# A second buffer for the small softmax weights, and ScalarE's exponentials ahead of its copies within each place

## The chip, the core and the metric

The kernel runs on one core of one Trainium2 chip. The metric is device time in microseconds (us), the median of several runs. Engines go by the profile's names: PE is TensorE (PEld its weight loads), ACT is ScalarE, DVE is VectorE, POOL is GpSimd, SP is the queue that issues the DMAs. "SPq", "ACTq" are the sequencers of those engines.

## The reference

A layer norm feeds two branches that are added to the input: latent attention and an int8 quantised feed-forward layer. What matters here is the attention:

```python
kv_c = x @ W_kv_down;  q_c = x @ W_q_down          # latents, rank 64 and 192
q = concat(q_c @ W_q_nope, rope(q_c @ W_q_rope))   # 16 heads
k = concat(kv_c @ W_k_nope, rope(kv_c @ W_k_rope)) # 4 key heads, each for 4 query heads
attn = softmax(where(causal, -inf, q @ k.T * scale))
out = (attn @ v) @ W_o                             # 2 sequences of 1024 tokens
```

## The kernel before

Each engine has its own program, written out by hand; the engines meet only at semaphores, and each works strictly through its list. After about 90 us of preparation comes the attention loop of 32 **steps** (n = 0 to 31), each one query head over one sequence of 1024 tokens, and then the feed-forward layer from about 760 us. The work of a step is cut into 7 **places** (j = 0 to 6).

The 1024 queries of a step are 8 tiles of 128 rows. Tile i sees (i + 1) * 128 keys. `UNITS` gives the tiles that a place handles: 7, 3, 6, 2, 5, then 1 and 0 together, then 4. Tiles 7, 6, 5, 4 are **big**: their scores alternate between two pairs of PSUM banks. Tiles 3, 2, 1, 0 are **small**: they all share one PSUM bank, so each small place can only be scored when DVE has finished with the one before it.

For one tile: PE forms the scores (`scores`, L1214); DVE takes the row maximum (`maxima`, L864); ACT exponentiates twice, once to an f16 high part in SBUF (L679 big, L684 small) and once in place in PSUM (L680, L685); DVE subtracts to get the f16 low part (`big_low` L872, `small_low` L879). Then SP turns the weights with DMA transposes (`turn_big` L358, `turn_small` L367) and PE multiplies them with the values one step later (tiles 6, 5, 4 and the small ones) or at place 6 of the same step (tile 7).

The high and low parts of all four small tiles of a step lie in one buffer, `p_small`, and go through one DMA transpose into `pt_small`. So the first small exponential of step n (tile 3, place 1) waits until the transpose of step n - 1 has landed (`small_in`, L683). That transpose is issued after the last `small_low` of step n - 1, which DVE does at the end of place 6.

Beside this, PE fills a bank `misc` with side work whose results another engine copies out; each new entry of `misc` waits for the copy of the last (`misc_used`). `misc_of(n)` lists it. With r = n % 4:

- every step (up to n = 29): two halves of a query for step n + 2, places 3 and 5, copied out by ACT (`query`, L608). POOL then rotates them.
- r = 0 or 2 (n from 2; 15 steps, below called **turn steps**): two transposes of normalised heads, `turn` 1 at place 5 and `turn` 0 at place 6. ACT copies each out (`turn_high`, L665) and DVE then makes the low part (`turn_low`, L898).
- r = 1 and r = 2 (n over 4): output products, two in each such step, added up by DVE (`add_out`); ACT has no part in them.
- in steps 0, 1, 3, 4, 7, 8, 11, 12 some extra entries (`EXTRA`): integer weights and activations that ACT copies out, and keys.

In the text, step 16 is the one whose first exponential starts at 432.54 us; it has r = 0. Step 17 starts at 454.39 and step 18 (r = 2) at 474.74.

Within place j, the lists read so. PE: scores of the place, products with values, then the `misc` entries. DVE at place 5: maxima of tiles 1 and 0, normalisation, low part of tile 5, `turn_low` 1. DVE at place 6: maximum of tile 4, `turn_low` 0, then `small_low` of tiles 1 and 0. At places 0 to 2 of the next step: maximum of 7, low part of 4, maximum of 3, maximum of 6, low part of 7, `small_low` of 3. ACT (L687 to L707): first the copies out of `misc` of the place, then its exponentials. PE's scores of tile 3 wait for `small_low` of tile 0, those of tile 6 for the low part of tile 4 of the step before, those of tile 2 (place 3) for `small_low` of tile 3.

Of the kernel before, what the change touches and what calls it, by code (L numbers as in the profile page):

```python
# [20 lines left out]
P = 128  # L21
# [26 lines left out]
F32, F32R, F16, BF16, U32 = (mybir.dt.float32, mybir.dt.float32r, mybir.dt.float16, mybir.dt.bfloat16,  # L48
                             mybir.dt.uint32)
ALU, ACT, AX = mybir.AluOpType, mybir.ActivationFunctionType, mybir.AxisListType  # L50
# [14 lines left out]
COLS = {7: 0, 5: 0, 6: 2 * CH, 4: 2 * CH + P, 3: 4 * CH, 2: 4 * CH, 1: 4 * CH, 0: 4 * CH + 2 * P}  # L65
KEYS = {7: (CH, CH), 6: (CH, CH - P), 5: (CH, 2 * P), 4: (CH - P, 2 * P), 3: (CH,), 2: (CH - P,), 1: (2 * P,), 0: (2 * P,)}

OFF = {3: 0, 2: 4 * P, 1: 7 * P, 0: 9 * P}
WB = 10 * P
# [5 lines left out]
QHI_SLOT = 4  # L75
# [11 lines left out]
LAST = HKV * STEPS  # L87


def misc_of(n):  # L90

    r, usual = n % REP, []
    if n + 2 < LAST:
        usual += [(3, "query", 0), (5, "query", 1)]
    if n < LAST:
        if r in (0, 2) and n >= 2:
            usual += [(5, "turn", 1), (6, "turn", 0)]
        if r == 1 and n > REP:
            usual += [(4, "out", 0), (6, "out", 1)]
        if r == 2 and n > REP:  # L100
            usual += [(2, "out", 2), (4, "out", 3)]
    return sorted(usual + EXTRA.get(n, []), key=lambda x: x[0])
# [8 lines left out]
def misc_index(n, kind, k):  # L111

    return MISC_BASE + MISC_AT[n, kind, k]


def build(nc, x, w_kv_down, w_k_nope, w_k_rope, w_v, w_q_down, w_q_nope, w_q_rope, w_o, w1, b1, w2, b2,
          cos_rows, sin_rows, out):
    with ExitStack() as ctx:
        def sb(name, shape, dt, where=ctx):
            return where.enter_context(nc.sbuf_tensor(name, shape, dt))  # L120

        def sem(name):
            return ctx.enter_context(nc.semaphore(name))
# [40 lines left out]
        psum = ctx.enter_context(nc.psum_tensor("psum", [P, 8 * CH], F32))  # L164
# [45 lines left out]
        att = ExitStack()  # L210
# [2 lines left out]
        q_raw = [sb(f"q_raw{i}", [P, T], F32, att) for i in range(2)]  # L213
        q_lo = [sb(f"q_lo{i}", [P, T], F32R, att) for i in range(2)]
        q_hi = [sb(f"q_hi{i}", [P, T], F32R, att) for i in range(2)]
        p_small = sb("p_small", [P, 2 * WB], F16, att)
        pt_small = sb("pt_small", [P, len(BLOCKS), P], F16, att)
        p_src = [sb(f"p_src{i}", [P, 2, T], F16, att) for i in range(PSRC)]
        pt_big = {i: sb(f"pt_big{i}", [P, 2 * (i + 1), P], F16, att) for i in BIG}
# [31 lines left out]
        S = {n: sem(n) for n in names}  # L251
# [27 lines left out]
        def _(sp):  # L279
# [87 lines left out]
            def turn_small(n):  # L367

                if n:
                    sp.wait_ge(S["pv_done"], PV_STEP * n)  # L370
                sp.wait_ge(S["small_lo"], len(SMALL) * (n + 1))
                sp.dma_start(pt_small[:, :, :], p_small[:, :], transpose=True).then_inc(S["small_in"], 16)

            for g in range(HKV):
                for s in range(STEPS):
                    n = STEPS * g + s
# [146 lines left out]
        def _(act):  # L523
# [84 lines left out]
            def query(n, s, idx, k):  # L608
                act.wait_ge(S["misc_full"], idx + 1)
                if k == 0 and n is not None:  # L610
                    act.wait_ge(S["qlo_done"], n - 1)
                act.activation(q_raw[s % 2][:, k * CH:(k + 1) * CH], misc[:, :], ACT.Copy, scale=SCALE)\  # L612
                   .then_inc(S["misc_used"], 1)

            def query_high(n, s):
                act.wait_ge(S["rotated"], n + 1)
                act.activation(q_hi[n % 2][:, :], q_raw[s % 2][:, :], ACT.Copy).then_inc(S["qhi_done"], 1)  # L617
# [6 lines left out]
            def turned_integers(kind, k, idx):  # L624
                act.wait_ge(S["misc_full"], idx + 1)
                if kind == "x":
                    ins = act.activation(qx_t[:, k % 2, k // 2 * CH:(k // 2 + 1) * CH], misc[:, :], ACT.Copy, bias=-MAGIC)
                elif k < 2:
                    ins = act.activation(w1_t[:, k, :], misc.bitcast(BF16), ACT.Copy)
                else:  # L630
                    ins = act.activation(w2_t[:, 4 * (k - 2):4 * (k - 1), :],
                                         misc.bitcast(BF16).rearrange("p (t n) -> p t n", n=D), ACT.Copy)
                ins.then_inc(S["misc_used"], 1)
# [35 lines left out]
            def exponentials(n, u):  # L669

                for i in UNITS[u]:
                    w, nb = (i + 1) * P, sm["mcol"][:, NT * (n % 2) + i:NT * (n % 2) + i + 1]
                    src = psum[:, COLS[i]:COLS[i] + w]
                    act.wait_ge(S["max_done"], NT * n + MAX_AT[UNITS[u][-1]] + 1)
                    if i in BIG:
                        q = NB * n + BIG[i]
                        if q >= PSRC:
                            act.wait_ge(p_in[q % PSRC], 32 * (q // PSRC))
                        act.activation(p_src[q % PSRC][:, 0, 0:w], src, ACT.Exp, bias=nb).then_inc(S["hi_done"], 1)  # L679
                        act.activation(src, src, ACT.Exp, bias=nb).then_inc(S["exp_done"], 1)  # L680
                    else:
                        if n:
                            act.wait_ge(S["small_in"], 16 * n)  # L683
                        act.activation(p_small[:, OFF[i]:OFF[i] + w], src, ACT.Exp, bias=nb)  # L684
                        act.activation(src, src, ACT.Exp, bias=nb).then_inc(S["small_exp"], 1)  # L685

            for n in range(LAST + 1):  # L687
                s = n % STEPS
                for j in range(NS):
                    for slot, kind, k in misc_of(n):  # L690
                        if slot != j:
                            continue
                        idx = misc_index(n, kind, k)
                        if kind == "query":
                            query(n + 2, s + 2, idx, k)
                        elif kind in ("w", "x"):
                            turned_integers(kind, k, idx)
                        elif kind == "turn":
                            turn_high(1 if s % REP == 0 else 0, k, idx)
                    if n == LAST:  # L700
                        continue
                    if j == QHI_SLOT and n + 1 < LAST:
                        query_high(n + 1, s + 1)
                    exponentials(n, j)
                    for slot, kind, k in misc_of(n):
                        if slot == j and kind == "kb":
                            keys_high(k)  # L707
            act.activation(sm["gelu"], sm["half"][:, 0:1], ACT.Gelu)

# [27 lines left out]
        def _(dve):  # L737
# [141 lines left out]
            def small_low(n, i):  # L879

                o, w = OFF[i], (i + 1) * P
                dve.wait_ge(S["small_exp"], len(SMALL) * n + SMALL[0 if i == 1 else i] + 1)
                dve.tensor_tensor(p_small[:, WB + o:WB + o + w], psum[:, COLS[i]:COLS[i] + w], p_small[:, o:o + w],  # L883
                                  ALU.subtract).then_inc(S["small_lo"], 1)

            def normalise(m, half):
# [89 lines left out]
            for n in range(LAST + 1):  # L976
                s, r = n % STEPS, n % REP
                for j in range(NS):
# [36 lines left out]
                    if n < LAST and j == 6:  # L1015
                        small_low(n, 1)
                        small_low(n, 0)
# [6 lines left out]
            for i in range(16):  # L1024
# [5 lines left out]
                if i in OUT_AT:  # L1030
                    k = OUT_AT[i]
# [424 lines left out]
```

## Time and profile before

| | |
|---|---|
| three runs | 828.88, 833.61, 837.66 us; median 833.61 |
| the profiled execution | 825.37 us, of which its span 823.6 us |
| mean granted TensorE clock | 0.915 |
| PE busy | 653.2 us (79%) |
| DVE busy | 551.5 us (67%) |
| ACT busy | 503.1 us (61%) |
| POOL busy | 417.7 us (51%) |

The span runs from the first to the last instruction of the profiled execution; the rest of its time lies around it. Busy shares are means over preparation, the attention loop and the feed-forward layer. In the loop no engine is busy throughout, so the waits between them decide.

### The profile page before, as it was taken

How to read it: one execution, taken by the hardware profiler on the slowest of the kernel's cores; microseconds unless marked ns; L12 is line 12 of the kernel's file. 1: busy time of each engine (PE TensorE's matmuls, PEld its weight loads, DVE VectorE, ACT ScalarE, POOL GpSimd, SP SyncE). 2: the span in 40 equal slices, each digit the busy share in tenths (PEclk: the TensorE clock that was granted, in tenths of full speed). 3: DMA queues.
4: the chain of work that ended last, by engine and by line, in shares of the span. 5: the costliest groups of instructions: out<-in, count | busy, mean ns of one | idle time of the engine just before them, and what ended most of it. 6: DMA issues, size and time to landing. Idle time of an engine off the chain costs nothing.

```text
span 823.6 us, 15788 instructions
## 1 busy us (share of the span) xinstructions
PE 653.2 (79%) x6282; PEld 509.1 (62%) x6282; DVE 551.5 (67%) x890; ACT 503.1 (61%) x759; POOL 417.7 (51%) x208
## 2 busy tenths in 40 slices
PE   8885778887888798878887887788877877886766
PEld 6663556665666576656765675566666755674535
DVE  6746687766677667765765677566665756676696
ACT  4556765676566656665666666566665657665553
POOL 2411656565566555564656565555564646540225
PEclk9776897999999999998989999999999999998879
DMA  9762468777958756785767758777676757668102
GB/s 274 239 215 119 84 131 143 128 145 174 179 97 150 146 113 110 155 148 120 129 116 141 117 116 149 134 129 129 123 133 112 120 97 133 118 117 147 30 1 103
DMA packets 323609, 108.34 MB, mean 132 GB/s; under 512 B 305808, under 2 KB 314576, under 8 KB 323408
## 3 DMA queue, kind: packets, MB, share of 16 engines
q1 hardware_dynamic: 322752, 106.74, 66.0%
q8 instruction: 50, 0.82, 0.4%
q10 hardware_dynamic: 784, 0.59, 0.3%
q14 instruction: 23, 0.19, 0.1%
HBM read 21.30 MB, written 10.49 MB: 39 GB/s over the span
## 4 chain that ended last, share of the span: by engine, by line
PE 49%; DVE 21%; DMA 14%; ACT 10%; issue 5%; POOL 0%; SPq 0%; POOLq 0%; ACTq 0%; DVEq 0%
PE psum L1077 45%; DMA pt_small<-p_small 11%; DVE small L868 5%; DVE p_small L883 3%; DVE p_src L876 3%; ACT psum L685 2%; DMA pt_big<-p_src 2%; PE psum L1275 2%; ACT p_src L679 2%; ACT psum L680 1%; DVE hid L1057 1%; ACT q_raw L612 1%; ACT p_small L684 1%; DVE kt_a L963 1%; DVE small L1026 1%
## 5 line engine op out<-in xcount | busy, mean ns | idle before, releaser
L868 DVE TENSOR_REDUCE small<-psum 128x1 f32<-128x1024 f32 (+7 forms) x256 | 188.9, 752 | 84.9 <-PE psum L1077 84.8
L486 POOL TENSOR_TENSOR q_lo<-q_raw,q_hi 128x1024 fp32r<-128x1024 f32 x32 | 76.5, 2390 | 242.0 <-ACT q_hi L617 242.0
L1077 PE MATMUL psum<-k_hi,q_hi 128*128 128x512 f32 (+2 forms) x384 | 165.4, 431 | 26.0 <-DVE p_src L876 18.0
L679 ACT ACTIVATE p_src<-psum,small 128x1024 f16<-128x1024 f32 (+3 forms) x128 | 122.1, 954 | 80.3 <-DVE small L868 79.8
L876 DVE TENSOR_TENSOR p_src<-psum,p_src 128x1024 f16<-128x1024 f32 (+3 forms) x128 | 130.0, 1016 | 12.5 <-ACT psum L680 12.4
L1077 PE MATMUL psum<-k_lo,q_hi 128*128 128x512 f32 (+2 forms) x384 | 135.7, 353 | 0.0
L1077 PE MATMUL psum<-k_hi,q_lo 128*128 128x512 f32 (+2 forms) x384 | 135.7, 353 | 0.0
L1077 PE MATMUL psum<-cmask,ident 128*128 128x128 bf16 x256 | 59.4, 232 | 87.9 <-DVE p_small L883 87.0
L680 ACT ACTIVATE psum<-psum,small 128x1024 f32<-128x1024 f32 (+3 forms) x128 | 118.5, 926 | 0.0
L883 DVE TENSOR_TENSOR p_small<-psum,p_small 128x512 f16<-128x512 f32 (+3 forms) x128 | 59.5, 486 | 86.0 <-ACT psum L685 85.1
L1077 PE MATMUL psum<-kv_tok,pt_big 128*128 128x65 f16 (+1 forms) x2496 | 106.8, 200 | 8.5 <-DMA pt_big<-p_src 8.4
L1077 PEld LDWEIGHTS psum<-kv_tok,pt_big 128*128 128x128 f16 x2496 | 90.7, 102 | 31.3 <-issue 20.9
L1077 PEld LDWEIGHTS psum<-cmask,ident 128*128 128x128 bf16 x256 | 24.7, 97 | 130.5 <-DVE p_small L883 93.9
L684 ACT ACTIVATE p_small<-psum,small 128x512 f16<-128x512 f32 (+3 forms) x128 | 67.8, 530 | 60.2 <-DMA pt_small<-p_small 50.6
L1077 PEld LDWEIGHTS psum<-k_hi,q_hi 128*128 128x128 f32 x384 | 78.1, 203 | 42.3 <-DVE p_src L876 27.5
L471 POOL TENSOR_TENSOR q_swap<-q_raw,sin_sb 32x1024 f32<-32x1024 f32 x31 | 73.4, 2368 | 48.3 <-ACT q_raw L612 33.8
L612 ACT ACTIVATE q_raw<-psum 128x512 f32<-128x512 f32 x64 | 38.3, 599 | 91.7 <-PE psum L1077 91.7
L1077 PEld LDWEIGHTS psum<-k_hi,q_lo 128*128 128x128 f32 x384 | 75.6, 197 | 7.5
L1077 PEld LDWEIGHTS psum<-k_lo,q_hi 128*128 128x128 f32 x384 | 76.7, 200 | 2.3
L480 POOL TENSOR_TENSOR q_raw<-q_raw,q_swap 64x1024 f32<-64x1024 f32 x31 | 74.7, 2410 | 2.4
L474 POOL TENSOR_TENSOR q_swap<-q_raw,sin_sb 32x1024 f32<-32x1024 f32 x31 | 73.9, 2384 | 2.4
L477 POOL TENSOR_TENSOR q_raw<-q_raw,cos_sb 64x1024 f32<-64x1024 f32 x31 | 73.3, 2363 | 2.4
(164 smaller groups left out, 1154.9 us busy)
## 6 DMA issues: line engine op xcount, KB each, us to landing
wq_split<-w_split SPq DMA_DIRECT2D x4, 1024.0 KB, 5.4
k_rotated<-k_split SPq DMA_DIRECT2D x8, 512.0 KB, 3.4
wq<-wq_split SPq DMA_DIRECT2D x16, 256.0 KB, 3.1
pt_big<-p_src SPq DMA_TRANSPOSE x256, 3.1
acc<-in_L_attn_x SPq DMA_DIRECT2D x4, 512.0 KB, 7.5
ffn_t<-in_L_attn_W_o SPq DMA_DIRECT2D x1, 2048.0 KB, 20.0
k_hi<-k_rotated SPq DMA_DIRECT2D x8, 256.0 KB, 4.0
k_lo<-k_rotated SPq DMA_DIRECT2D x8, 256.0 KB, 4.5
```

What stands on the lines that cost most here:

```text
L471: pool.tensor_tensor(q_swap[0:HR, :], raw[HR:ROPE, :], sin_sb[HR:ROPE, :], ALU.mult)\
L474: pool.tensor_tensor(q_swap[HR:ROPE, :], raw[0:HR, :], sin_sb[0:HR, :], ALU.mult)\
L477: pool.tensor_tensor(raw[0:ROPE, :], raw[0:ROPE, :], cos_sb[0:ROPE, :], ALU.mult)\
L480: pool.tensor_tensor(raw[0:ROPE, :], raw[0:ROPE, :], q_swap[:, :], ALU.add).then_inc(S["pool_step"], 1)
L486: pool.tensor_tensor(q_lo[s % 2][:, :], q_raw[s % 2][:, :], q_hi[n % 2][:, :], ALU.subtract)\
L679: act.activation(p_src[q % PSRC][:, 0, 0:w], src, ACT.Exp, bias=nb).then_inc(S["hi_done"], 1)
L680: act.activation(src, src, ACT.Exp, bias=nb).then_inc(S["exp_done"], 1)
L684: act.activation(p_small[:, OFF[i]:OFF[i] + w], src, ACT.Exp, bias=nb)
L868: dve.tensor_reduce(sm["mcol"][:, NT * (n % 2) + i:NT * (n % 2) + i + 1], psum[:, COLS[i]:COLS[i] + (i + 1) * P], AX.X, ALU.max, negate=True)\
L876: dve.tensor_tensor(p_src[q % PSRC][:, 1, 0:w], psum[:, COLS[i]:COLS[i] + w], p_src[q % PSRC][:, 0, 0:w], ALU.subtract).then_inc(S["lo_don ...
L883: dve.tensor_tensor(p_small[:, WB + o:WB + o + w], psum[:, COLS[i]:COLS[i] + w], p_small[:, o:o + w], ALU.subtract).then_inc(S["small_lo"], 1)
L1077: ins = pe.matmul(dst, lhs, rhs, start=start, stop=stop, skip_group_check=True)
```

## The change

Two edits. First, `p_small` becomes two buffers, used in turn by the parity of the step; the first small exponential of step n now waits for the transpose of step n - 2. `pt_small`, the transpose itself and its place in SP's list stay as they are. Second, ACT does the exponentials of a place first (preceded at place 4 by `query_high`, as before) and then the copies out of `misc`; the keys' high part stays behind the exponentials.

```diff
-        p_small = sb("p_small", [P, 2 * WB], F16, att)
+        p_small = [sb(f"p_small{k}", [P, 2 * WB], F16, att) for k in range(2)]
...
-                sp.dma_start(pt_small[:, :, :], p_small[:, :], transpose=True).then_inc(S["small_in"], 16)
+                sp.dma_start(pt_small[:, :, :], p_small[n % 2][:, :], transpose=True).then_inc(S["small_in"], 16)
...
-                        if n:
-                            act.wait_ge(S["small_in"], 16 * n)
-                        act.activation(p_small[:, OFF[i]:OFF[i] + w], src, ACT.Exp, bias=nb)
+                        if n >= 2:
+                            act.wait_ge(S["small_in"], 16 * (n - 1))
+                        act.activation(p_small[n % 2][:, OFF[i]:OFF[i] + w], src, ACT.Exp, bias=nb)
...
             for n in range(LAST + 1):
                 s = n % STEPS
                 for j in range(NS):
+                    if n < LAST:
+                        if j == QHI_SLOT and n + 1 < LAST:
+                            query_high(n + 1, s + 1)
+                        exponentials(n, j)
                     for slot, kind, k in misc_of(n):
                         if slot != j:
                             continue
...
                             turn_high(1 if s % REP == 0 else 0, k, idx)
-                    if n == LAST:
-                        continue
-                    if j == QHI_SLOT and n + 1 < LAST:
-                        query_high(n + 1, s + 1)
-                    exponentials(n, j)
-                    for slot, kind, k in misc_of(n):
-                        if slot == j and kind == "kb":
+                        elif kind == "kb":
                             keys_high(k)
...
-                dve.tensor_tensor(p_small[:, WB + o:WB + o + w], psum[:, COLS[i]:COLS[i] + w], p_small[:, o:o + w],
+                dve.tensor_tensor(p_small[n % 2][:, WB + o:WB + o + w], psum[:, COLS[i]:COLS[i] + w], p_small[n % 2][:, o:o + w],
```

The lists of PE, DVE, SP and POOL keep their order. ACT's changes. In a turn step, ACT's places 5 and 6 read like this before: the second half of a query is copied (`q_raw`), then `turn` 1 (`o_hi`), then the exponentials of tiles 1 and 0 (`p_small` is a high part in SBUF, `psum` the one in place), then `turn` 0, then tile 4.

```order
L612 ACTIVATE q_raw<-psum 128x512 [waits misc_full]
L667 ACTIVATE o_hi<-psum 128x512 [waits misc_full]
L684 ACTIVATE p_small<-psum,small 128x256 [waits small_in,max_done]
L685 ACTIVATE psum<-psum,small 128x256
L684 ACTIVATE p_small<-psum,small 128x128 [waits small_in,max_done]
L685 ACTIVATE psum<-psum,small 128x128
L667 ACTIVATE o_hi<-psum 128x512 [waits misc_full]
L679 ACTIVATE p_src<-psum,small 128x640 [waits p_in2,max_done]
L680 ACTIVATE psum<-psum,small 128x640
```

The same two places of ACT now:

```order
L684 ACTIVATE p_small<-psum,small 128x256 [waits small_in,max_done]
L685 ACTIVATE psum<-psum,small 128x256
L684 ACTIVATE p_small<-psum,small 128x128 [waits small_in,max_done]
L685 ACTIVATE psum<-psum,small 128x128
L612 ACTIVATE q_raw<-psum 128x512 [waits misc_full]
L667 ACTIVATE o_hi<-psum 128x512 [waits misc_full]
L679 ACTIVATE p_src<-psum,small 128x640 [waits p_in2,max_done]
L680 ACTIVATE psum<-psum,small 128x640
L667 ACTIVATE o_hi<-psum 128x512 [waits misc_full]
```

The exponentials of tiles 1 and 0 moved ahead of two copies, and the copy of `turn` 0 moved behind those of tile 4. DVE's list at the same places, the same before and now, is what takes from these: low part of tile 5, `turn_low` 1 (`o_lo`), maximum of tile 4, `turn_low` 0, `small_low` of tiles 1 and 0, then the maximum of tile 7 of the next step and the low part of tile 4.

```order
L876 TENSOR_TENSOR p_src<-psum,p_src 128x768 [waits exp_done]
L901 TENSOR_TENSOR o_lo<-psum,o_hi 128x512 [waits o_hi_done]
L868 TENSOR_REDUCE small<-psum 128x1 [waits score_done]
L901 TENSOR_TENSOR o_lo<-psum,o_hi 128x512 [waits o_hi_done]
L883 TENSOR_TENSOR p_small<-psum,p_small 128x256 [waits small_exp]
L883 TENSOR_TENSOR p_small<-psum,p_small 128x128 [waits small_exp]
L868 TENSOR_REDUCE small<-psum 128x1 [waits score_done]
L876 TENSOR_TENSOR p_src<-psum,p_src 128x640 [waits exp_done]
```

Nothing moved here. At place 3 of every step with a query, ACT had the copy of its first half ahead of tile 2; this is before:

```order
L612 ACTIVATE q_raw<-psum 128x512 [waits qlo_done,misc_full]
L684 ACTIVATE p_small<-psum,small 128x384 [waits small_in,max_done]
L685 ACTIVATE psum<-psum,small 128x384
L617 ACTIVATE q_hi<-q_raw 128x1024 [waits rotated]
L679 ACTIVATE p_src<-psum,small 128x768 [waits p_in2,max_done]
```

And the same place of ACT now:

```order
L684 ACTIVATE p_small<-psum,small 128x384 [waits small_in,max_done]
L685 ACTIVATE psum<-psum,small 128x384
L612 ACTIVATE q_raw<-psum 128x512 [waits qlo_done,misc_full]
L617 ACTIVATE q_hi<-q_raw 128x1024 [waits rotated]
L679 ACTIVATE p_src<-psum,small 128x768 [waits p_in2,max_done]
```

The two exponentials of tile 2 moved ahead of the copy; `query_high` and tile 5 follow as before.

## Rows read from the trace of the kernel before

**Rows 1.** The page, part 4: the chain that ended last, by line.

```profile
PE psum L1077 45%; DMA pt_small<-p_small 11%; DVE small L868 5%; DVE p_small L883 3%; DVE p_src L876 3%; ACT psum L685 2%; DMA pt_big<-p_src 2%; PE psum L1275 2%; ACT p_src L679 2%; ACT psum L680 1%; DVE hid L1057 1%; ACT q_raw L612 1%; ACT p_small L684 1%; DVE kt_a L963 1%; DVE small L1026 1%
```

**Rows 2.** Waits: who waited for whom, us in total, times, longest.

```profile
POOL q_lo L486 <- ACT q_hi L617: 242.0, 32, 13.9
...
PE psum L1077 <- DVE p_small L883: 87.0, 34, 4.8
...
ACT p_small L684 <- DMA pt_small<-p_small: 50.6, 24, 3.6
```

**Rows 3.** Timeline, step 16, places 0 to 3: start, us, engine, [idle before <-releaser].

```profile
433.55 1.08 ACT L680 ACTIVATE psum<-psum,small 128x1024 f32<-128x1024 f32 x1
...
435.95 1.22 DVE L876 TENSOR_TENSOR p_src<-psum,p_src 128x1024 f16<-128x1024 f32 x1
...
436.70 0.69 ACT L684 ACTIVATE p_small<-psum,small 128x512 f16<-128x512 f32 x1 [2.07 <-DMA pt_small<-p_small]
...
437.97 0.69 DVE L883 TENSOR_TENSOR p_small<-psum,p_small 128x512 f16<-128x512 f32 x1 [0.80 <-ACT psum L685]
...
438.72 0.29 PE L1077 MATMUL psum<-cmask,ident 128*128 128x128 bf16 x1 [3.24 <-DVE p_small L883]
```

**Rows 4.** Groups by line and shape: busy us, mean ns, idle before, releaser.

```profile
L883 DVE TENSOR_TENSOR p_small<-psum,p_small 128x512 f16<-128x512 f32 x32 | 22.0, 688 | 16.7 <-ACT psum L685 16.4
...
L883 DVE TENSOR_TENSOR p_small<-psum,p_small 128x384 f16<-128x384 f32 x32 | 17.9, 558 | 68.9 <-ACT psum L685 68.7
```

**Rows 5.** Timeline, step 16 (r = 0), places 5 and 6, ACT.

```profile
447.74 0.60 ACT L612 ACTIVATE q_raw<-psum 128x512 f32<-128x512 f32 x1
449.14 0.60 ACT L667 ACTIVATE o_hi<-psum 128x512 fp32r<-128x512 f32 x1 [0.81 <-PE psum L1275]
449.64 0.47 ACT L684 ACTIVATE p_small<-psum,small 128x256 f16<-128x256 f32 x1
...
450.60 0.36 ACT L685 ACTIVATE psum<-psum,small 128x128 f32<-128x128 f32 x1
451.37 0.60 ACT L667 ACTIVATE o_hi<-psum 128x512 fp32r<-128x512 f32 x1 [0.41 <-PE psum L1275]
451.87 0.79 ACT L679 ACTIVATE p_src<-psum,small 128x640 f16<-128x640 f32 x1
452.54 0.77 ACT L680 ACTIVATE psum<-psum,small 128x640 f32<-128x640 f32 x1
```

**Rows 6.** Timeline, the same stretch, DVE.

```profile
445.17 1.48 DVE L868 TENSOR_REDUCE small<-psum 128x1 f32<-128x768 f32 x3
...
450.38 0.81 DVE L868 TENSOR_REDUCE small<-psum 128x1 f32<-128x640 f32 x1
452.00 0.69 DVE L901 TENSOR_TENSOR o_lo<-psum,o_hi 128x512 fp32r<-128x512 f32 x1 [0.81 <-ACT o_hi L667]
452.61 0.61 DVE L883 TENSOR_TENSOR p_small<-psum,p_small 128x256 f16<-128x256 f32 x2
453.14 1.22 DVE L868 TENSOR_REDUCE small<-psum 128x1 f32<-128x1024 f32 x1
```

**Rows 7.** Timeline, step 17, PE: the scores of tiles 6 and 2.

```profile
455.14 0.50 PE L1077 MATMUL psum<-k_hi,q_hi 128*128 128x512 f32 x1 [0.82 <-DVE p_src L876]
...
460.35 0.23 PE L1077 MATMUL psum<-cmask,ident 128*128 128x128 bf16 x1 [3.02 <-DVE p_small L883]
```

**Rows 8.** Timeline, step 18 (r = 2), place 5, ACT and DVE.

```profile
487.37 0.62 DVE L868 TENSOR_REDUCE small<-psum 128x1 f32<-128x256 f32 x2 [0.26 <-PE psum L1077]
...
488.63 0.60 ACT L612 ACTIVATE q_raw<-psum 128x512 f32<-128x512 f32 x1 [0.59 <-PE psum L1077]
```

**Rows 9.** Windows: us, busy of each engine, PEclk, DMA share, GB/s.

```profile
412.44:432.54 20.10, 16.44 (x162) 12.98 (x162) 12.42 (x21) 12.47 (x20) 9.89 (x5) 0.83 0.67 119
495.28:513.27 17.99, 13.91 (x162) 10.94 (x162) 12.32 (x21) 12.47 (x20) 9.59 (x5) 1.00 0.87 153
...
99.00:760.00 661.00, 535.08 (x5617) 424.51 (x5615) 444.53 (x713) 416.65 (x641) 366.03 (x156) 0.94 0.72 132
```

## The prediction

> **What bounds the kernel now.** I read the chain that ended last first, for the engine and the stall on it: PE's matmuls (L1077) are 45% of the span and the transpose of the small weights is 11%, by far the largest piece that is not computing [rows 1]. Next the waits, for who is late to whom: ACT idles 50.6 us in 24 places for that transpose, and PE idles 87.0 us in 34 places for `small_low` (L883), mostly before the scores of tile 2 [rows 2]. So the naive reading is that one buffer costs up to 50.6 us. Then I read one such stall in time order, because a wait is worth only what the next engine does with it.
>
> In step 16 ACT is done with tile 7 at 433.55 + 1.08 = 434.63, could start tile 3 then, and starts at 436.70 [rows 3]. But DVE takes tile 3 only after the low part of tile 7, which ends at 435.95 + 1.22 = 437.17. It started `small_low` at 437.97, with 0.80 us of true idle before it, and PE followed at 438.72 after 3.24 us idle [rows 3]. Of ACT's 2.07 us wait, PE can get 0.80 back. The rest is covered by DVE, whose own work since the scores of tile 6 is the true chain to PE.
>
> **The second buffer (term A).** Over the kernel, DVE's idle before `small_low` of tile 3 is 16.7 us, of which ACT is blamed for 16.4 [rows 4]. With two buffers ACT can be ready before DVE in every step: from 434.63, two exponentials up to the 1.27 us that lie between 436.70 and DVE's start at 437.97 end at 435.90, ahead of 437.17 [rows 3]. So A = -16.4 us. Its bounds are 0 (something else late takes its place) and -50.6 us (all of ACT's wait [rows 2]); I take the DVE row, since PE waits for DVE and not for ACT. The transpose still goes out at the same time, so what SP has queued behind it (the two transposes of tile 4, for PE's products right after the scores of tile 2) gets no earlier.
>
> The Trainium skill speaks for the change: the page "Trainium Kernel Development and Optimization", section Best Practices, tells to double-buffer so that DMA overlaps with compute. By it the DMA wait would vanish, 50.6 us; by DVE's idle row it is worth 16.4 us here, since another engine stands between the buffer and PE.
>
> **Exponentials first at place 3.** Today DVE idles 68.7 us before `small_low` of tile 2 [rows 4], about 2.1 us in each of 32 steps, because ACT waits for the query's matmuls and copies before it exponentiates. The new order removes most of that. What is behind it on DVE is the maximum of tile 5, then the maxima of 1 and 0 that wait for PE's next scores; and PE's wait row for L883 counts 34 stalls in 32 steps, about one a step, the one at tile 2 [rows 2, 7]. PE does not wait for tile 2's low part (which gates tiles 1 and 0). I cost it at nothing: PE's own queue of matmuls hides it. The copy comes later by the two exponentials only where PE's matmuls were done before; POOL, which takes queries onward, idles 242.0 us [rows 2], 7.6 us a step, and hides a delay of under 2 us.
>
> **Exponentials first at places 5 and 6 of a turn step (term B).** Here DVE's list alternates with ACT's: `turn_low` 1, maximum of 4, `turn_low` 0, `small_low` 1 and 0, maximum of 7. Step 16 by its rows [rows 5, 6]:
>
> - Maxima of 5, 1, 0 end at 445.17 + 1.48 = 446.65. New: the four exponentials start there. They took 449.64 to 450.60 + 0.36 = 450.96, so 1.32 us; the copy of the query can start about 447.9 against 447.74 now. All that follows up to `turn_low` 1 and the maximum of 4 shifts by 0.1 to 0.2 us.
> - The maximum of 4 ends at 450.38 + 0.81 = 451.19, now near 451.35. New: ACT does tile 4 at once, two activations of 0.67 us start to start (451.87 to 452.54), and only then the copy of `turn` 0: 451.4 + 1.35 = 452.75, where it was 451.37. Shift 1.4 us.
> - DVE waits for that copy to do `turn_low` 0 (452.00) and, behind it, `small_low` 1 and 0 (452.61) and the maximum of 7 (453.14). All shift by 1.4 us. No idle lies before the maximum of 7 in which it could be lost.
> - PE's scores of tile 3 wait for that `small_low`; those of tile 6 wait for the low part of 4, right behind the maximum of 7, and already waited (455.14, 0.82 idle) [rows 7]. Then maximum of 6, low part of 7, `small_low` 3, scores of 2: the stall of 3.02 us at 460.35 [rows 7] stays, 1.4 us later, less the gain of A.
>
> For r = 2 the first point is worse. Maxima of 1 and 0 end at 487.37 + 0.62 = 487.99 and the copy of the query starts at 488.63 [rows 8]; new it starts at 487.99 + about 1.25 = 489.25, 0.6 us later, so `turn_low` 1 is 0.6 us later and the total 0.6 + 1.25 = 1.85 us. There are 7 turn steps with r = 0 and 8 with r = 2: B = 7 x 1.4 + 8 x 1.85 = 24.6 us. Bounds: 15 x 0.8 = 12 us, if the 0.8 us idle ahead of tile 6 swallows part, and 15 x 2.1 = 32 us, if both copies are delayed by both pairs.
>
> **Smaller terms.** C: a few transposes land late (longest ACT wait 3.6 us against 2.07 in step 16 [rows 2, 3]). Where this falls on the step after a turn, tile 4's transposes, queued on SP behind an even later small one, keep PE from its products, so about 1.5 us of A is lost twice: 3 us, between 0 and 5. D: twelve copies of integer activations and weights in steps 0 to 4 fall behind exponentials. Where two `misc` entries follow each other PE waits for the copy; a pair of 0.67 us activations is 1.3 us. I take three such delays, 4 us, between 0 and 12 x 1.3 = 16 us. The feed-forward part is not touched.
>
> **Sum.** -16.4 + 24.6 + 3 + 4 = +15.2 us. Against the profiled execution: 825.4 + 15.2 = 840.6 us, 1.8% more. The median of the three runs is 833.6, 1.0% over that execution, so I forecast 833.6 + 15.2 = 849 us.
>
> **TensorE's clock.** The granted clock was 0.94 over the loop [rows 9], a mix of the two levels 1.2 and 2.4 GHz: (1 - 0.94) / 0.5 x 661 = 79 us at the lower. Two steps with the same work show its price: 20.10 us at 0.83 and 17.99 us at 1.00, so 6.8 us at 1.2 GHz cost 2.1 us [rows 9]; by that rate the loop pays 79 x 0.31 = 24 us. The idle before tile 2 shrinks (3.24 to about 2.4 us) while new idle before tile 3 comes up in turn steps. I take no change, and half of the 24 us either way as the bound. The Trainium skill, page "TensorE: Matmul & The Clock Gate", section "Why this matters for your kernels", says that idle gaps between bursts of matmuls bring the lower clock. The stall of 3.24 us fits it, with a slower mask (0.29 us) behind it [rows 3]; the one of 3.02 us, with 0.23 us behind it [rows 7], does not.
>
> **The rivals.**
>
> 1. The buffer decides (faster). If the copy of `turn` 0 slips without delaying DVE, only A is left: 833.6 - 16.4 = 817 us, and it would be lower still by the double-buffering rule. For it: 11% of the chain is this transpose [rows 1]. Against it: DVE stands idle for exactly that copy (0.81 us at 452.00 [rows 6]). It decides from the point where the shift of a turn step is under (16.4 - 7) / 15 = 0.6 us. Chance 0.12.
> 2. The clock gives back (no change). Shorter stalls keep 2.4 GHz longer and save 12 us: 833.6 + 3 = 837 us. For it: the longest stalls are the ones that shrink. Against it: a turn step has more idle in all. Chance 0.16.
> 3. The clock takes more. Each turn step has a stall at tile 3, at tile 6 and at tile 2 within a few us, and the lower clock is granted 12 us' worth more: 861 us. Chance 0.15.
> 4. Half and half: turn steps lose only 0.8 us each and A is whole, D small: -16.4 + 12 + 4 = 0, so 834 us. Chance 0.07.
>
> **Numbers.** The forecast (841 to 858 us) has 0.50. Time over 1% either way (under 825.3 or over 841.9) is about what a measurement of this kernel can tell from no change. Faster is rival 1 and a sliver of rival 2: 0.13. Same is the rest of rival 2 and rival 4: 0.22. Slower is the forecast and rival 3: 0.65. The range leaves out rival 1 and the far end of rival 3: 829 to 863 us. The forecast's own range is 841 to 858.
>
> **What the changed profile would show.** A right: no ACT wait for `pt_small` left, and DVE's idle before `small_low` 128x512 near 0; PE's stall before tile 2 near 2.4 us. B right: in turn steps `o_hi` of `turn` 0 starts 1.3 us or more behind the maximum of 4, behind both activations of 128x640; DVE's waits for `o_hi` grow from 0.8 us to over 2 us in each; PE shows a new stall before the scores of tile 3. Place 3 right: the 68.7 us of DVE idle before 128x384 shrink by more than half, and the time shows nothing of it. The forecast is wrong if DVE turns out to have slack behind `turn_low` 0, if tile 2's earliness shortens the way to place 5 by more than the copies lose, or if the granted clock over the loop moves away from 0.94.

## The result

The changed kernel takes 858.76 us (median of 4 runs, 854.11 to 860.86) against 832.59 us before: the ratio is 1.030, 95% interval 1.023 to 1.0375. It is slower by 26 us; the forecast was 849 us, slower by 15. The profiled execution took 857.32 us, its span is 855.5 us, its mean granted clock 0.892 where it was 0.915. In the experiments below, times are medians, and executions that ran slow at a lower granted clock are left out of them.

The page of the changed kernel, part 4 (the chain that ended last, by line). From L706 of the kernel before on, the line numbers are lower by 2: L881 is `small_low`, L874 `big_low`, L866 the maxima, L899 `turn_low`, L1075 the matmuls, L1273 the `turn` transposes.

```profile
PE psum L1075 47%; DVE small L866 11%; DVE p_src L874 6%; DVE p_small L881 3%; ACT psum L680 2%; DVE o_lo L899 2%; DMA pt_big<-p_src 2%; ACT o_hi L667 2%; DVE hid L1055 1%; PE psum L1273 1%; ACT psum L685 1%; ACT q_raw L612 1%; ACT p_small L684 1%; DVE small L1024 1%; DVE kt_a L961 1%
```

The transpose of the small weights, 11% in [rows 1], has left the chain. DVE's maxima and low parts stand in its place. The waits of the changed kernel (us in total, times, longest):

```profile
PE psum L1075 <- DVE p_small L881: 79.1, 44, 4.7
DVE o_lo L899 <- ACT o_hi L667: 58.2, 31, 2.0
...
PE psum L1273 <- ACT q_raw L612: 21.8, 14, 2.4
...
PE psum L1324 <- ACT ffn_t L627: 6.5, 3, 2.8
```

PE's wait for `small_low` fell only from 87.0 us to 79.1, and it now comes 44 times instead of 34 [rows 2]: twelve of them are stalls of about 1 us before the scores of tile 3, by the timeline. `turn_low` now waits 58.2 us for ACT's copies; in the kernel before, this wait and the one of `turn`'s transposes for the copy of the query were:

```profile
DVE o_lo L901 <- ACT o_hi L667: 25.8, 28, 1.3
...
PE psum L1275 <- ACT q_raw L612: 16.0, 14, 1.4
```

Two groups of the changed kernel by line and shape, the ones that answer to [rows 4] (busy, mean ns, idle before):

```profile
L881 DVE TENSOR_TENSOR p_small<-psum,p_small 128x512 f16<-128x512 f32 x32 | 21.7, 679 | 0.0
...
L881 DVE TENSOR_TENSOR p_small<-psum,p_small 128x384 f16<-128x384 f32 x32 | 17.8, 557 | 2.7
```

Both idle times, 16.7 and 68.9 us before, are gone, as the two edits mean them to be. The kernel is slower all the same.

### The profile page after: what moved, and what is told of

It reads as the page before. It is cut to its first block, busy times and chain, and to the rows that moved or that the text cites. A ratio compares the mean times of both kernels' runs of the same rounds, so it can differ in the third digit from the quotient of the medians.

```text
span 855.5 us, 15781 instructions
## 1 busy us (share of the span) xinstructions
PE 673.9 (79%) x6279; PEld 521.8 (61%) x6282; DVE 552.1 (65%) x890; ACT 507.5 (59%) x759; POOL 416.5 (49%) x208
## 4 chain that ended last, share of the span: by engine, by line
PE 50%; DVE 30%; ACT 11%; issue 5%; DMA 3%; SPq 0%; POOL 0%; POOLq 0%; DVEq 0%; ACTq 0%
PE psum L1075 47%; DVE small L866 11%; DVE p_src L874 6%; DVE p_small L881 3%; ACT psum L680 2%; DVE o_lo L899 2%; DMA pt_big<-p_src 2%; ACT o_hi L667 2%; DVE hid L1055 1%; PE psum L1273 1%; ACT psum L685 1%; ACT q_raw L612 1%; ACT p_small L684 1%; DVE small L1024 1%; DVE kt_a L961 1%
## 5 line engine op out<-in xcount | busy, mean ns | idle before, releaser
L866 DVE TENSOR_REDUCE small<-psum 128x1 f32<-128x1024 f32 (+7 forms) x256 | 190.2, 753 | 156.5 <-PE psum L1075 154.9
L1075 PE MATMUL psum<-k_hi,q_hi 128*128 128x512 f32 (+2 forms) x384 | 170.1, 443 | 25.8 <-DVE p_src L874 17.8
L1075 PE MATMUL psum<-k_lo,q_hi 128*128 128x512 f32 (+2 forms) x384 | 139.4, 363 | 0.0
L1075 PE MATMUL psum<-k_hi,q_lo 128*128 128x512 f32 (+2 forms) x384 | 139.4, 363 | 0.0
L874 DVE TENSOR_TENSOR p_src<-psum,p_src 128x1024 f16<-128x1024 f32 (+3 forms) x128 | 129.7, 1013 | 1.4 <-ACT psum L680 1.4
L1075 PE MATMUL psum<-cmask,ident 128*128 128x128 bf16 x256 | 60.5, 236 | 79.1 <-DVE p_small L881 79.1
L1075 PE MATMUL psum<-kv_tok,pt_big 128*128 128x65 f16 (+1 forms) x2496 | 107.2, 200 | 9.4 <-DMA pt_big<-p_src 9.3
L1075 PEld LDWEIGHTS psum<-kv_tok,pt_big 128*128 128x128 f16 x2496 | 91.1, 102 | 33.4 <-issue 18.6
L1075 PEld LDWEIGHTS psum<-k_hi,q_hi 128*128 128x128 f32 x384 | 81.4, 212 | 41.8 <-DVE p_src L874 28.2
L1075 PEld LDWEIGHTS psum<-cmask,ident 128*128 128x128 bf16 x256 | 25.4, 99 | 125.3 <-DVE p_small L881 86.0
L1075 PEld LDWEIGHTS psum<-k_hi,q_lo 128*128 128x128 f32 x384 | 78.0, 203 | 8.2
L1075 PEld LDWEIGHTS psum<-k_lo,q_hi 128*128 128x128 f32 x384 | 79.4, 207 | 2.7
L1075 PE MATMUL psum<-qc_hi,wq 128*128 128x512 f32 x128 | 66.8, 522 | 6.0 <-ACT ffn_t L629 2.0
L685 ACT ACTIVATE psum<-psum,small 128x512 f32<-128x512 f32 (+3 forms) x128 | 64.7, 505 | 0.0
```

The source lines that it names most:

```text
L866: dve.tensor_reduce(sm["mcol"][:, NT * (n % 2) + i:NT * (n % 2) + i + 1], psum[:, COLS[i]:COLS[i] + (i + 1) * P], AX.X, ALU.max, negate=True)\
L874: dve.tensor_tensor(p_src[q % PSRC][:, 1, 0:w], psum[:, COLS[i]:COLS[i] + w], p_src[q % PSRC][:, 0, 0:w], ALU.subtract).then_inc(S["lo_don ...
L1075: ins = pe.matmul(dst, lhs, rhs, start=start, stop=stop, skip_group_check=True)
```

## The profile after, at the places of the prediction

Timeline of the changed kernel, step 16, places 1 to 3 (answers to [rows 3]):

```profile
459.81 0.69 ACT L684 ACTIVATE p_small<-psum,small 128x512 f16<-128x512 f32 x1
460.38 0.67 ACT L685 ACTIVATE psum<-psum,small 128x512 f32<-128x512 f32 x1
...
461.22 1.22 DVE L874 TENSOR_TENSOR p_src<-psum,p_src 128x1024 f16<-128x1024 f32 x1
...
462.35 0.68 DVE L881 TENSOR_TENSOR p_small<-psum,p_small 128x512 f16<-128x512 f32 x1
...
463.09 0.23 PE L1075 MATMUL psum<-cmask,ident 128*128 128x128 bf16 x1 [2.35 <-DVE p_small L881]
```

ACT is done with tile 3 at 461.05, 1.3 us before DVE takes it, DVE goes straight from tile 7 to tile 3, and PE's stall is 2.35 us instead of 3.24, as the prediction's 2.4 said.

Timeline of the same step, places 5 and 6 and the start of step 17 (answers to [rows 5, 6, 7]):

```profile
472.16 0.63 ACT L612 ACTIVATE q_raw<-psum 128x512 f32<-128x512 f32 x1
...
472.94 0.63 PE L1273 MATMUL psum<-identf,o_norm 128*128 128x128 f32 x4 [1.56 <-ACT q_raw L612]
473.60 0.60 ACT L667 ACTIVATE o_hi<-psum 128x512 fp32r<-128x512 f32 x1 [0.81 <-PE psum L1273]
...
474.84 0.81 DVE L866 TENSOR_REDUCE small<-psum 128x1 f32<-128x640 f32 x1
475.69 0.79 ACT L679 ACTIVATE p_src<-psum,small 128x640 f16<-128x640 f32 x1 [1.49 <-DVE small L866]
...
477.05 0.60 ACT L667 ACTIVATE o_hi<-psum 128x512 fp32r<-128x512 f32 x1
477.68 0.69 DVE L899 TENSOR_TENSOR o_lo<-psum,o_hi 128x512 fp32r<-128x512 f32 x1 [2.03 <-ACT o_hi L667]
...
478.96 0.23 PE L1075 MATMUL psum<-cmask,ident 128*128 128x128 bf16 x1 [0.99 <-DVE p_small L881]
```

The copy of `turn` 0 starts 1.40 us after the end of tile 4's maximum (474.84 + 0.81 = 475.65 to 477.05); before, it was 0.18 us (451.19 to 451.37). DVE waits 2.03 us for it instead of 0.81, and so it does in each of the 15 turn steps; PE has a stall of 0.99 us before tile 3 that it did not have.

Windows of the changed kernel, steps 0 to 4 and steps 5 to 30 (us, busy times, PEclk, DMA share, GB/s):

```profile
92.49:216.01 123.52, 91.95 (x839) 70.34 (x837) 78.95 (x119) 74.46 (x113) 65.02 (x29) 0.88 0.59 110
216.01:774.11 558.10, 456.48 (x4666) 360.23 (x4666) 363.76 (x587) 343.66 (x523) 306.81 (x132) 0.93 0.69 128
```

The same windows of the kernel before:

```profile
88.26:193.77 105.51, 85.12 (x839) 65.91 (x837) 78.11 (x119) 73.15 (x114) 64.28 (x29) 0.92 0.72 129
193.77:742.00 548.23, 445.85 (x4666) 354.26 (x4666) 363.86 (x587) 340.60 (x522) 308.27 (x132) 0.95 0.72 131
```

Steps 0 to 4 lost 18.0 us, the 26 steps 5 to 30 lost 9.9 us. That is where the forecast's sum was off, and where the experiments began. Another 4.2 us of the difference between the two profiles lie ahead of the loop (it starts at 88.26 us before and at 92.49 now), where no instruction was changed; they belong to these two executions and not to the change (see the last section).

## The experiments

All of them have two buffers unless the text says otherwise. ACT's loop is written so that one condition decides, for each step n and place j, whether the exponentials go first; the kernels differ in that condition. The kernel before was measured again beside each group of kernels: 830.3 us beside the ones with the buffers alone, the order alone, place 6 and steps 5 to 31; 829.6 beside the copies of integers, places 5 and 3 and the first late `turn_low`; 831.3 beside the other four; and 832.6 beside the changed kernel. A difference between kernels of two groups is uncertain by these 2 to 3 us.

```diff
+                    exp_first = ...
+                    if not exp_first:
+                        copies()
                     if n < LAST:
                         if j == QHI_SLOT and n + 1 < LAST:
                             query_high(n + 1, s + 1)
                         exponentials(n, j)
+                    if exp_first:
+                        copies()
```

### Each edit alone

The buffer alone, with ACT's order of before:

```diff
+                    exp_first = False
```

> Two buffers for the small weights, with ScalarE's order of before. My sum: the second buffer alone gives back DVE's idle ahead of small_low of tile 3, 16.4 us, so 832.6 - 16 = about 816 us, with no ACT wait for pt_small left and that DVE idle near zero. Rival (the double-buffering rule read plainly): all 50.6 us of ACT's wait, about 782 us. Rival (a late landing of tile 4's transposes, queued on SP behind the small one, takes the wait's place): within 4 us of before.

Measured: 814.9 us against 830.3 before, ratio 0.981 (0.976 to 0.987). That is 15.4 us less (11 to 20 by the interval), the DVE idle row of [rows 4] and not the ACT wait row of [rows 2]. `pt_small` no longer shows in the waits.

The order alone, one buffer:

```diff
+                    exp_first = True
...
-        p_small = [sb(f"p_small{k}", [P, 2 * WB], F16, att) for k in range(2)]
+        p_small = [sb(f"p_small{k}", [P, 2 * WB], F16, att) for k in range(1)]
```

with `p_small[0]` everywhere and the wait of before.

> One buffer as before, ScalarE's new order everywhere. If the two edits add up, this is the changed kernel less the buffer's gain: 858.8 + 16 = about 875 us. Rival (the new order makes the buffer worthless or the reverse, since the transpose goes out later in turn steps): the same as the changed kernel, 859 us, or over 880 us because the turn steps' delay now also reaches the first small exponential.

Measured: 867.6 us, ratio 1.046 (1.040 to 1.052). Waits of this kernel:

```profile
ACT p_small L684 <- DMA pt_small<-p_small: 45.0, 25, 3.6
DVE p_small L889 <- ACT psum L685: 12.4, 17, 2.3
```

The order costs 37 us by itself (830.3 to 867.6). With it the buffer is worth 8.9 us (867.6 to 858.8), not 15.4; DVE's idle before `small_low` of tile 3 is 12.5 us here and was 16.7. The two edits don't quite add.

### Where in the loop the order costs

The new order in steps 5 to 31 only (`n >= 5`):

> The changed kernel with ScalarE's order of before in steps 0 to 4, the ones with the copies of integers. The two profiles put 18 us of the loss into these five steps where my term D said 4. If that is the order of the integer copies, this kernel takes 858.8 - 13 or so, 843 to 848 us. Rival (it was the granted clock of that one execution, 30.7 us at 1.2 GHz there against 17.1): the same as the changed kernel less 4 us, 855 us.

Measured: 838.3 us, ratio 1.0095 (1.005 to 1.014). So the order costs 838.3 - 814.9 = 23.4 us in the 27 later steps and 858.8 - 838.3 = 20.5 us in the first five. The lengths of the steps in the two profiles (from first exponential to first exponential, n from 5 on) say where the 23.4 us lie: the six turn steps with r = 0 grow from 21.1 to 22.7 us, the seven with r = 2 from 20.2 to 22.0, 22 us in all.

The new order at place 6 of every step (`j == 6`), and at place 6 of steps 5 to 31 (`n >= 5 and j == 6`):

> Two buffers, ScalarE's exponentials ahead of its copies at place 6 only (the turn 0 copy behind tile 4's exponentials, 15 times, and three copies of integers in steps 0 and 3). My sum: 15 turn steps by 1.3 us is 20 us over the kernel with the buffers alone, so about 816 + 20 = 836 us, DVE waits for o_hi up by some 20 us. Rival (DVE has slack behind turn_low 0): no more than 5 us over the kernel with the buffers alone.

> Two buffers, exponentials first at place 6 of steps 5 to 31 only, so that the 13 copies of turn 0 alone are moved behind tile 4. By my steps 13 x 1.35 = 17.5 us over the kernel with the buffers alone, so 832 us; with the integer copies of steps 0 and 3 included it was 842.4. Rival (the whole of that 27.5 us is the turn copies): 840 us.

Measured: 842.4 us and 834.1 us. Thirteen copies of `turn` 0 cost 19.2 us over the buffers alone, 1.5 us each, where my steps gave 1.35. The remaining 8.3 us come, by subtraction, from two turn steps and three copies of integers at place 6 of steps 0 and 3, more than I had said.

The new order only at the eleven places in steps 0, 1, 3 and 4 that hold copies of integers:

```diff
+                    exp_first = (n, j) in {(0, 2), (0, 4), (0, 6), (1, 4), (3, 0), (3, 1), (3, 2), (3, 4), (3, 6), (4, 0), (4, 1)}
```

> Two buffers, ScalarE's exponentials ahead of its copies only at the 11 places of steps 0, 1, 3 and 4 that hold copies of integer weights and activations (one of them, place 4 of step 0, also has the high part of a query ahead of it in either order). The changed kernel lost 20.5 us in steps 0 to 4 against the same kernel with the old order there (858.8 against 838.3). If the integer copies are it, this takes 814.9 + 15 to 20 = 830 to 835 us. Rival (the query and turn copies of those steps, as in the rest of the loop, about 1 us a step, and the clock): 818 to 821 us.

Measured: 830.75 us, 15.9 us over the buffers alone. Timeline of this kernel, step 3, places 0 to 5; places 0, 1, 2 and 4 have such a copy (`ffn_t`, L627):

```profile
161.84 1.08 ACT L680 ACTIVATE psum<-psum,small 128x1024 f32<-128x1024 f32 x1
162.83 0.60 ACT L627 ACTIVATE ffn_t<-psum 128x512 bf16<-128x512 f32 x1
...
163.49 0.66 PE L1332 MATMUL psum<-identf,acc 128*128 128x128 f32 x4 [2.25 <-ACT ffn_t L627]
...
165.54 1.09 DVE L874 TENSOR_REDUCE small<-psum 128x1 f32<-128x896 f32 x1 [3.42 <-PE psum L1083]
...
178.30 0.51 PE L1083 MATMUL psum<-qc_hi,wq 128*128 128x512 f32 x1 [2.29 <-ACT ffn_t L627]
```

PE stands 2.25 us for a copy that is queued behind tile 7's maximum and both its exponentials, and 2.29 us again behind tile 5. Nothing stands in for it, since the scores of the next tile are behind the transpose on PE's list, and DVE and then ACT wait in turn (3.42 us on DVE). All of PE's waits for such copies in this kernel, where with the buffers alone they are 1.3 us in two places:

```profile
PE psum L1332 <- ACT ffn_t L627: 5.9, 3, 2.3
PE psum L1083 <- ACT ffn_t L629: 2.8, 2, 2.4
...
PE psum L1083 <- ACT ffn_t L631: 2.3, 1, 2.3
PE psum L1083 <- ACT ffn_t L627: 2.3, 1, 2.3
```

That is 13.3 us in seven places, most of the 15.9.

### Places 5 and 3

Place 5 alone (`j == 5`) and place 3 alone (`j == 3`), in all steps:

> Two buffers, exponentials first at place 5 only, in all steps (ahead of the second half of a query and of turn 1). By my steps the copy of the query comes 0.15 us later in 7 turn steps and 0.6 us in 8, and nothing else hangs on it: 814.9 + 6 = 821 us. Rival (place 5 is free, all of the turn steps' loss is at place 6): 815 us. Rival (PE waits for the query's copy in every step): over 827 us.

> Two buffers, exponentials first at place 3 only: tile 2 ahead of the copy of the first half of a query. I costed it at nothing: 814.9 us within 2, while DVE's idle before the 128x384 small_low falls from about 69 us to under 35. Rival (DVE's 2.1 us a step are worth something to PE): 808 us or less.

Measured: 840.6 us and 802.9 us. Both expectations fell, in opposite directions: place 5 alone costs 25.7 us and place 3 alone gains 12.0 us over the buffers alone. Timelines of step 16 at place 5: with the buffers alone,

```profile
447.38 0.87 ACT L680 ACTIVATE psum<-psum,small 128x768 f32<-128x768 f32 x1
448.16 0.60 ACT L612 ACTIVATE q_raw<-psum 128x512 f32<-128x512 f32 x1
...
448.91 0.63 PE L1281 MATMUL psum<-identf,o_norm 128*128 128x128 f32 x4 [1.43 <-ACT q_raw L612]
```

with place 5 changed,

```profile
461.05 0.87 ACT L680 ACTIVATE psum<-psum,small 128x768 f32<-128x768 f32 x1
...
463.04 0.63 ACT L612 ACTIVATE q_raw<-psum 128x512 f32<-128x512 f32 x1
...
463.82 0.63 PE L1281 MATMUL psum<-identf,o_norm 128*128 128x128 f32 x4 [2.37 <-ACT q_raw L612]
```

and with place 3 changed:

```profile
433.04 0.60 ACT L612 ACTIVATE q_raw<-psum 128x512 f32<-128x512 f32 x1 [0.38 <-PE psum L1083]
...
433.78 0.63 PE L1281 MATMUL psum<-identf,o_norm 128*128 128x128 f32 x4 [0.78 <-ACT q_raw L612]
```

In a turn step PE waits at place 5 for the copy of the query before it may transpose. With r = 0 and the buffers alone, the copy waits for tile 5's exponentials, which wait for tile 5's maximum, which on DVE stands behind `small_low` of tile 2. So an early tile 2 does reach PE: the stall falls from 1.43 to 0.78 us, and ACT now waits 0.38 us for PE instead of PE's product waiting for ACT. The copy starts 12.05 us after the step's first exponential instead of 13.07, and all behind it comes as much earlier: step 16 takes 18.7 us instead of 19.7. With r = 2 nothing is gained: there the copy already waits for PE, as in [rows 8], and the stall is 0.78 us in both kernels. The mean lengths of the steps from n = 5 on agree: 21.1 to 19.2 us for the six with r = 0, 20.2 and 20.2 for the seven with r = 2.

Place 5 puts four more exponentials ahead of that copy and the stall rises to 2.37 us. Its cost, too, lies mostly in the steps with r = 0: they grow from 21.1 to 24.3 us, where I expected 0.15 us more, and the ones with r = 2 from 20.2 to 20.8, the 0.6 us that I expected. In the changed kernel both act, and the stall is 1.56 us: place 3's gain is spent at place 5.

### Taking the cause away on DVE's side

The new order in steps 5 to 31, with DVE's `turn_low` 0 moved behind the maximum of 7 and the low part of 4 of the next step, so that nothing PE waits for stands behind the late copy:

```diff
-                        if kind == "turn":
+                        if kind == "turn" and (k == 1 or n < 5):
                             turn_low(1 if r == 0 else 0, k, TURNS[n] + 2 - k)
...
                     if n and j == 0:
                         big_low(n - 1, 4)
+                    if n > 5 and j == 0 and (n - 1, "turn", 0) in MISC_AT:
+                        turn_low(1 if (n - 1) % REP == 0 else 0, 0, TURNS[n - 1] + 2)
```

> The kernel with the new order in steps 5 to 31 (838.3 us), with one more change: DVE does turn_low 0 not ahead of small_low 1 and 0 at place 6 but behind the maximum of 7 and the low part of 4 of the next step, so that nothing on DVE that PE waits for stands behind ScalarE's late copy. If that serial chain is the whole cost of place 6, 13 turn steps get 1.25 to 1.4 us back: 838.3 - 17 = 821 us. Rival (PE or ScalarE is late for another reason): 834 us or more.

Measured: 813.3 us against 838.3 with ACT's list the same: 25.0 us back, more than the 17 expected. By the lengths of the steps, the turn steps get 1.4 us each back (r = 0: 22.7 to 21.2; r = 2: 22.0 to 20.6), 18.6 us for the thirteen, which leaves them 0.1 and 0.4 us longer than with the buffers alone. So the chain on DVE behind `turn` 0 is most of the cost of the order in the loop. The other 6 us lie outside the turn steps; the mean granted clock rose from 0.904 to 0.917 with it, and no run says whether that is their cause. The same move without the late copy at place 6 brings little (the second kernel below), so it is not a gain that would have come anyway.

### Towards a better version

From the kernel with two buffers and place 3 (802.9 us): DVE's `small_low` of tile 3 ahead of the low part of tile 7 at place 2; the late `turn_low` 0; and both.

```diff
-                            big_low(n, 7)
-                            small_low(n, 3)
+                            small_low(n, 3)
+                            big_low(n, 7)
```

> Two buffers, exponentials first at place 3 (802.9 us), and DVE does small_low of tile 3 ahead of the low part of tile 7 at place 2 instead of behind it. If DVE's own order is now what PE's stall before tile 2 consists of, PE could start 1.2 us earlier in each step, 35 us in all; but the transposes of tile 4 that PE needs next land about 1 us behind tile 2's scores of now, so I expect 0.2 to 0.4 us a step: 792 to 797 us. Rival (all of it): 768 us. Rival (a later low part of tile 7 delays its transposes and tile 5's scores): 803 us or more.

> Two buffers, exponentials first at place 3 (802.9 us), and DVE's turn_low 0 behind the maximum of 7 and the low part of 4 of the next step in steps 6 to 30. DVE waits 0.8 us for ScalarE's copy there now; if small_low and the maximum of 7 can go ahead, 13 turn steps gain 0.6 to 1.4 us each: 785 to 795 us. Rival (PE's scores are what DVE would wait for next): 801 to 803 us.

> Both of the last two changes of DVE's order on the kernel with two buffers and place 3. If they work on different stalls their gains add; then this is the fastest kernel, about 785 us. Rival (both run into the landing of tile 4's transposes): no faster than the better of the two.

Measured: 782.6 us (ratio 0.938, 0.932 to 0.945), 797.7 us (0.957, 0.949 to 0.966) and 771.0 us (0.922, 0.912 to 0.932). The swap gives 20 us, more than I allowed. What the late `turn_low` 0 gives by itself is not clear: 797.7 us stands on two executions, with 810.0 and 813.1 beside them, against 802.9, and steps 5 to 30 take 517.5 us in its profile instead of 519.9; its own forecast, 785 to 795 us, was missed. Together with the swap it gives 11.5 us. Timeline with the swap, step 16, place 3:

```profile
413.50 0.23 PE L1083 MATMUL psum<-cmask,ident 128*128 128x128 bf16 x1 [1.22 <-DVE p_small L889]
...
415.08 0.63 PE L1083 MATMUL psum<-kv_tok,pt_big 128*128 128x65 f16 x15 [0.77 <-DMA pt_big<-p_src]
```

PE's stall before tile 2 is 1.22 us instead of 2.35, and 0.77 us come back as a wait for tile 4's transposes. The cap that I expected is there, but smaller than I said: over the kernel PE's wait for `small_low` falls from 67.3 to 34.5 us, and its wait for `pt_big` rises from 9.9 to 33.1. With the late `turn_low` 0 the latter is 21.7 us, less by as much as the time. The last kernel beats both kernels of this case, by 7.8% the one before.

## Why the prediction was right, and where its sum was not

The direction, the range (829 to 863 us) and the mechanism of A and B held. The forecast's own range (841 to 858 us) ends just below the 858.8 us measured, and a part of the match inside B is luck. Term by term:

| term | forecast, us | measured, us | by |
|---|---|---|---|
| A, the buffer | -16.4 | -15.4 | 830.3 to 814.9 |
| B in steps 5 to 31 (6 x 1.4 + 7 x 1.85), with C | +21.4 + 3 | +23.4 | 814.9 to 838.3 |
| D and B's two turn steps among steps 0 to 4 | +4 + 3.2 | +20.5 | 838.3 to 858.8 |
| sum | +15.2 | +28.5 | (+26.2 between the kernels' medians) |

- **A was right** within its interval, and so was the reason: PE waits for DVE and not for ACT, so the worth of the buffer is DVE's idle time. The Trainium skill (page "Trainium Kernel Development and Optimization", section Best Practices) tells to double-buffer and gives no price; read as the whole DMA wait it would have been 50.6 us. The rule holds in its direction.
- **B was right** in place 6, in its chain and in its sum: 1.40 us from the maximum to the copy where I said 1.4, no idle on DVE to swallow it, and 25 us back when that chain was cut. Turn steps grew by 1.6 us (r = 0, forecast 1.4) and 1.8 us (r = 2, forecast 1.85).
- **B's step at place 5 with r = 0 was wrong**, and luck covered it. I let the four exponentials start at 446.65 us, where the maxima end, and so moved the copy by 0.15 us. But ACT was not free then; it had just begun tile 5 (the kernel before, step 16):

```profile
446.16 0.90 ACT L679 ACTIVATE p_src<-psum,small 128x768 f16<-128x768 f32 x1 [1.07 <-DVE small L868]
446.95 0.87 ACT L680 ACTIVATE psum<-psum,small 128x768 f32<-128x768 f32 x1
```

  The four can start only at about 447.7 us, and all of their 1.3 us come before the copy. Place 5 alone costs 3.2 us in such a step. Place 3, which I put at nothing, gives 1.9 us of it back.
- **C** was not seen: over the kernel PE's wait for `pt_big` is 9.3 us where it was 8.4, so 1 us shows in place of 3.
- **D is the step that failed.** I priced a delayed copy of integers at a pair of 0.67 us activations and counted three. A run shows 15.9 us for these copies alone; the copies at the big tiles stand behind the maximum and two activations of about 1 us, PE's stalls are 2.25 and 2.29 us, and PE stands for such a copy in seven of the eleven places (13.3 us) and not in three. My upper bound for D, 16 us, was about what came (15.9 us); the value within it was not worked out by a place of its own, as B was.
- **Place 3 at nothing was wrong.** Alone it gains 12.0 us. I followed DVE's list from `small_low` 2 to the maximum of tile 5, said that PE's scores hide it, and stopped; the next releases (tile 5's exponentials, the query's copy, PE's transposes) were not followed, though I used the same earlier time in B. In the changed kernel place 5 takes it back, which is why the sum did not show the fault.
- **The clock term** was put at zero. Over 66 runs of the thirteen changed kernels here, taken within each kernel, time and mean granted clock go together: 5.7 us less for each 0.01 more (correlation -0.91). The four runs of the changed kernel are at 0.883 to 0.898, ten of the kernel before at 0.894 to 0.913, means 0.890 and 0.906. By that slope about 9 of the 26 us come with the clock. They are not in addition to the table: each difference there has its share. Rival 3, whose 861 us are nearer to the measured time than the forecast, therefore had something to it, and the profile's two windows show it (0.88 and 0.93 where they were 0.92 and 0.95). Whether the idle caused all of that clock or the clock differs for other reasons too stays open; no run here fixed the clock.
- Rival 1 fell: the order alone costs 37 us. Rival 2 (the clock gives back) went the other way. Rival 4 (turn steps lose 0.8 us each) fell at 1.6 to 1.8.

## What to carry to other kernels

Price an edit by the idle time of the engine that the bounding engine waits for, not by the wait that the edit removes: a 50.6 us wait was worth 15.4. When the order on one engine changes, look at every other engine's list for an item that waits for a moved result and has something urgent behind it; where such an item sits, moving it on the other engine (25 us here) can be worth more than the order itself. Split a reorder by place before judging it: here one place gained 12 us and two others lost 26 and 28.

## What the runs showed of the hardware

The lower clock does not follow from the length of a stall alone. In step 0 PE has the same stall of 2.49 us before tile 2 in two kernels, whose work up to that point on PE is the same. This is the kernel with the buffers alone:

```profile
98.70 0.23 PE L1083 MATMUL psum<-cmask,ident 128*128 128x128 bf16 x1 [2.49 <-DVE p_small L889]
98.73 0.42 PE L1083 MATMUL psum<-k_hi,q_hi 128*128 128x384 f32 x1
```

And this the changed kernel:

```profile
98.48 0.29 PE L1075 MATMUL psum<-cmask,ident 128*128 128x128 bf16 x1 [2.49 <-DVE p_small L881]
98.53 0.67 PE L1075 MATMUL psum<-k_hi,q_hi 128*128 128x384 f32 x1
```

The stalls end 0.2 us apart. One goes on at 2.4 GHz (0.42 us for the matmul, granted clock 1.00 from 98 to 99 us), the other at 1.2 GHz (0.67 us, granted clock 0.50). The preparation ahead of the loop, the same in every kernel here, shows it too: it takes 88.26 us at a granted clock of 0.79 in the profile of the kernel before, and 92.69 us at 0.74 with the buffers alone. Up to the end of step 0 ACT's and PE's order is the same in five of the kernels; it comes at 105.9 to 106.0 us in three profiles (before, steps 5 to 31, place 6 of steps 5 to 31) and at 110.3 to 110.4 us in two (buffers alone, the first late `turn_low`). So a difference of 4 us between two profiles can be chance, which is why the table above goes by medians. That the 1% between executions of one kernel is mostly this fits the slope above and is not shown. The page "TensorE: Matmul & The Clock Gate" of the Trainium skill, section "Part 1: The HAM clock gate (the "warmup" mystery)", calls the ramp at a kernel's start run-variable; no row here is of the start itself, but these, from the preparation and the first step, vary in the same way.
